# Layer 0 of a four-layer convolution kernel: planes without border rows, packed taps, results phase by phase, and sums in row halves

## The reference, cut to what matters

```python
base = conv1x1(x, w_qkv)                                  # 192 -> 576 channels
qkv = concatenate([dwconv(base, w_dw3, 1), dwconv(base, w_dw5, 2),
                   dwconv(base, w_dw7, 3)], axis=1)        # depthwise, 3 x 576 channels
qkv = conv1x1(qkv, w_pconv)                                # 1728 -> 576 channels
q, k, v = split(qkv, 3)                                    # 8 heads of 24 channels
q, k = l2norm(q), l2norm(k)                                # over the 4096 pixels
attn = einsum('bhcn,bhdn->bhcd', q, k) * temperature
# three softmaxes over the top 12, 16 and 18 of 24, mixed, times v, then w_proj
```

## Time and profile before

| | |
|---|---|
| median of 3 runs | 3204.47 us |
| profiled execution, its own time | 3192.12 us |
| its span (first to last instruction) | 3190.3 us |
| PE busy | 2387.6 us (75%) |
| DVE busy | 1220.4 us (38%) |
| ACT busy | 978.0 us (31%) |
| POOL busy | 812.5 us (25%) |
| transfers | 314.40 MB, mean 99 GB/s |
| mean granted clock of TensorE | 0.862 |

### The profile page before, as it was taken

The page is one execution under the profiler, slowest core; times in us unless marked ns, Lnnn a source line. Parts: engine busy times, 40 slices in busy tenths (PEclk is TensorE's granted clock), DMA queues, the critical chain, the costliest instruction groups (busy, mean ns, idle before and its releaser), DMA issues. The chain is left out here.

```text
span 3190.3 us, 37429 instructions
## 1 busy us (share of the span) xinstructions
PE 2387.6 (75%) x15968; PEld 1379.6 (43%) x15968; DVE 1220.4 (38%) x1081; ACT 978.0 (31%) x1264; POOL 812.5 (25%) x321
## 2 busy tenths in 40 slices
PE   3877878739999999995697938678677877877022
PEld 1566666627777777772352112223132212321022
DVE  4333434310000000004402160799499728974722
ACT  2344444410000000002210011666367526650400
POOL 1433334300000000000000000578188607870310
PEclk9989989869999999997795565799899989998556
DMA  5899999962122112102000110000000000002389
GB/s 180 273 296 310 292 302 283 267 225 86 49 90 90 65 70 90 45 1 84 9 1 29 46 48 20 0 0 0 0 1 0 0 0 1 0 16 66 107 226 272
DMA packets 175035, 314.40 MB, mean 99 GB/s; under 512 B 7049, under 2 KB 130185, under 8 KB 166217
## 3 DMA queue, kind: packets, MB, share of 16 engines
q1 hardware_dynamic: 162216, 305.94, 31.4%
q10 hardware_dynamic: 12672, 6.29, 0.7%
HBM read 185.59 MB, written 125.04 MB: 97 GB/s over the span
## 5 line engine op out<-in xcount | busy, mean ns | idle before, releaser
L589 PE MATMUL ps<-mem 128*128 128x288 f16 x5376 | 677.0, 286 | 50.9 <-DMA mem<-depthwise_out 50.9
L589 PEld LDWEIGHTS ps<-mem 128*128 128x128 f16 x5376 | 519.3, 98 | 194.5 <-issue 66.5
L1350 POOL TENSOR_TENSOR mem<-mem 128x1024 f32<-128x1024 f32 x48 | 113.1, 2356 | 1632.9 <-ACT mem L1340 1632.9
L1353 POOL TENSOR_TENSOR mem<-mem 128x1024 f32<-128x1024 f32 x192 | 448.3, 2353 | 40.8 <-ACT mem L1324 40.5
L434 PE MATMUL ps<-mem 56*96 56x256 f16 x5184 | 325.7, 288 | 105.8 <-DVE mem L527 96.4
L1298 PE MATMUL ps<-mem 128*128 128x512 f32 x768 | 379.3, 617 | 16.1 <-POOL mem L1353 13.2
L434 PEld LDWEIGHTS ps<-mem 56*96 56x96 f16 x5184 | 312.0, 130 | 127.4 <-DVE mem L527 102.8
L1381 DVE TENSOR_TENSOR_SCAN mem<-mem,ps 128x1024 f32<-128x1024 f32 x144 | 337.9, 2347 | 60.7 <-ACT mem L1331 37.2
L804 DVE MEMSET mem<- 96x96 f32 x2 | 0.3, 138 | 860.9 <-DMA mem<-in_tri 860.9
L527 DVE TENSOR_TENSOR mem<-ps,mem 96x1024 f16<-96x1024 f32 x144 | 171.3, 1217 | 274.6 <-ACT mem L472 274.6
L503 POOL TENSOR_TENSOR mem<-mem 120x2304 f16<-120x2304 f32 x36 | 163.7, 4548 | 342.0 <-ACT mem L465 342.0
(11 more groups left out here) (179 smaller groups left out, 2392.2 us busy)
## 6 DMA issues: line engine op xcount, KB each, us to landing
depthwise_out<-mem SPq DMA_DIRECT2D x36, 1536.0 KB, 15.6
mem<-depthwise_out SPq DMA_DIRECT2D x16, 3328.0 KB, 10.9
mem<-in_wd SPq DMA_DIRECT2D x40, 1080.0 KB, 17.4
mem<-base_phases SPq DMA_DIRECT2D x72, 504.0 KB
base_phases<-mem SPq DMA_DIRECT2D x56, 576.0 KB, 10.5
mem<-l_planes SPq DMA_DIRECT2D x48, 252.0 KB
mem<-in_x SPq DMA_DIRECT2D x4, 2048.0 KB, 10.9
l_planes<-mem SPq DMA_DIRECT2D x2, 4032.0 KB, 13.3
```

Source lines behind the costliest of these rows:

```text
L589: ins = nc.tensor.matmul(ps[:, 2 * (i % 2) + h, 0:HALF], d, pw[0:rows, wa, k, HALF * h:HALF * h + HALF], start=(k == 0 and n == 0), stop=( ...
L1353: nc.gpsimd.tensor_tensor(hh[:, n % 4, :], hh[:, n % 4, :], cs[:, n % 2, :], ALU.mult).then_inc(hc_pool, 1)
```

## The change

In layer 0's depthwise stage
- planes have 128 elements and no border rows (a row of 4 planes is 1024 instead of 1152 bytes). The matmuls for o = 0 and o = 2 leave out the block row that lies outside (240 instead of 256 columns) and come behind o = 1;
- taps are sent as 192 instead of 288 columns per channel pair: 96 for o = 1 and the 96 that are not zero in o = 0 and o = 2. Two transfers over 56 partitions each replace one over 120. ACT and POOL spread them with four instructions each where there was one. DVE clears the rest once;
- results are stored phase by phase, `[PHASES, 3 * QKV, 512]`, in three transfers over 32 partitions with runs of 16 KB;
- the second base matmul of each image uses only its 64 rows, and the two images' stand next to each other, on different rows of the array. The first 8 steps use three pairs of PSUM banks. In the loop the two steps of a batch stand ahead of units 0 and 2.

In the pointwise stage
- a piece comes in six transfers with runs of 1024 bytes; the last 64 rows are loaded twice, to both halves of the partitions, and the two output halves of the last row block use one half each;
- Gram sums are only q k'. DVE squares q and k of each block and adds the squares up; 8 matmuls with a column of ones behind the last block give the norms, and attention reads them.

Attention reads v in another order of phases. The diff, cut:

```diff
-        base_d = nc.dram_tensor("base_phases", [QKV, TAPROWS, PITCH], F16).ap()
-        d_dram = nc.dram_tensor("depthwise_out", [3 * QKV, PHASES, 4 * BLOCKS], F16).ap()
+        base_d = nc.dram_tensor("base_phases", [QKV, TAPROWS, PITCH0], F16).ap()
+        d_dram = nc.dram_tensor("depthwise_out", [PHASES, 3 * QKV, 4 * BLOCKS], F16).ap()
...
+    def base_before(n, k):
+        steps = base_steps(n)
+        return steps[k // 2:k // 2 + 1] if k % 2 == 0 else []
...
+    def base_psum(m, g, b):
+        return ps[0:width(m), (2 * (g % 3) if m == 0 else 0) + b, :]
...
             def load_taps(n):
-                sp.dma_start(w32[n % 2][0:64 + TAPROWS], inp["wd"][:, n * BP * YS * MD:(n + 1) * BP * YS * MD]).then_inc(w_loaded[n % 2], 16)
+                for t in range(2):
+                    sp.dma_start(w32[n % 2][64 * t:64 * t + TAPROWS], inp["wd"][TAPROWS * t:TAPROWS * (t + 1), n * BP * TAPS0:(n + 1) * BP * TAPS0]
+                                 ).then_inc(w_loaded[n % 2], 16)
...
             def store_out(n):
                 sp.wait_ge(dw_lo, UPB * (n + 1))
-                sp.dma_start(d_dram[6 * BP * n:6 * BP * (n + 1)].rearrange("(c k) f n -> (k f) c n", k=3), stg[n % 2][0:MD]
-                             ).then_inc(d_stored[n % 2], 16)
+                for k in range(3):
+                    sp.dma_start(d_dram[:, QKV * k + 2 * BP * n:QKV * k + 2 * BP * (n + 1)], stg[n % 2][PHASES * k:PHASES * (k + 1)]
+                                 ).then_inc(d_stored[n % 2], 16)
...
                 for b in range(B):
-                    nc.tensor.matmul(out, w[:, 0, c0:c0 + width(m)], xn[:, b, x], start=True, stop=False)
-                    nc.tensor.matmul(out, w[:, 1 + b, c0:c0 + width(m)], xn[:, 2, x], start=False, stop=True).then_inc(base_sum, 1)
+                    nc.tensor.matmul(base_psum(m, g, b), w[:, 0, c0:c0 + width(m)], xn[:, b, x], start=True, stop=False)
+                for b in range(B):
+                    p = slice(64 * b, 64 * b + 64)
+                    nc.tensor.matmul(base_psum(m, g, b), w[p, 1, c0:c0 + width(m)], xn[p, 2, x], start=False, stop=True).then_inc(base_sum, 1)
...
-                    for o in range(YS):
+                    for o in (1, 0, 2):
+                        lo, hi = 8 * (o == 0), BLOCKS - 8 * (o == 2)
...
             def taps(n):
+                src, dst = dense_taps(n)
+                nc.scalar.copy(dst[0], src).then_inc(w_hi, 1)
+                for q in range(3):
+                    src, dst = edge_taps(n, q)
+                    nc.scalar.copy(dst[0], src).then_inc(w_hi, 1)
...
-                src = d_dram[:, 2 * j:2 * j + 2, :].rearrange("c f n -> c (f n)")
-                sp.dma_start(dbuf[:, j % NSLOT, 0:NK - 1], src[0:128 * (NK - 1)].rearrange("(k p) n -> p k n", p=128)
-                             ).then_inc(d_loaded[j % NSLOT], 16)
-                sp.dma_start(dbuf[0:64, j % NSLOT, NK - 1], src[128 * (NK - 1):3 * QKV]).then_inc(d_loaded[j % NSLOT], 16)
+                for f in range(2):
+                    src, dst = d_dram[2 * j + f], dbuf[:, j % NSLOT, :, 512 * f:512 * f + 512]
+                    sp.dma_start(dst[:, 0:NK - 1], src[0:128 * (NK - 1)].rearrange("(k p) n -> p k n", p=128)).then_inc(d_loaded[j % NSLOT], 16)
+                    for h in range(2):
+                        sp.dma_start(dst[64 * h:64 * h + 64, NK - 1], src[128 * (NK - 1):3 * QKV]).then_inc(d_loaded[j % NSLOT], 16)
...
                         for h in range(2):
+                            rows = slice(64 * h, 64 * h + 64) if k == NK - 1 else slice(0, 128)
...
-                    pair = x[:, 0:2 * C].rearrange("p (a c) -> p a c", a=2)[:, :, h * HC:(h + 1) * HC]
-                    nc.tensor.matmul(ps[0:HC, 4 + 2 * b, 2 * HC * h:2 * HC * (h + 1)].rearrange("p (a c) -> p a c", a=2),
-                                     x[:, h * HC:(h + 1) * HC], pair, start=(f == 0 and h == 0), stop=(f == PHASES - 1), skip_group_check=True)
-                    ks = x[:, C + h * HC:C + (h + 1) * HC]
-                    ins = nc.tensor.matmul(ps[0:HC, 5 + 2 * b, HC * h:HC * (h + 1)], ks, ks,
+                    ins = nc.tensor.matmul(ps[0:HC, 4 + b, HC * h:HC * h + HC], x[:, h * HC:(h + 1) * HC], x[:, C + h * HC:C + (h + 1) * HC],
...
+                nc.vector.tensor_tensor(sq[:, i % 2], qkv[:, i % 2], qkv[:, i % 2], ALU.mult).then_inc(squared, 1)
+                dve.wait_ge(squared, i + 1)
+                nc.vector.tensor_tensor(sqsum[:, i % 2], sqsum[:, i % 2], sq[:, i % 2], ALU.add).then_inc(sq_added, 1)
```

More of the change, by code:

```diff
@@ L38 @@
 PITCH = 4 * PLANE
+PITCH0 = 4 * BLOCKS
+TAPS0 = 2 * MD
 SHIFTED = [0, 1, 2, 5, 6, 7]
@@ L278, in layer0_depthwise @@
     NM, NSTB, NWIN = 5, 4, 3
[L279 to L284, removed]
+    w = ar.take(2, QKV)
+    stb = ar.take16(NSTB, 4, PITCH0, dt=F16)
+    ext = ar.take16(len(SHIFTED), 4, PITCH0, dt=F16)
+    win = ar.take16(NWIN, BP, PITCH0, dt=F16)
+    WB = BP * YS * MD
+    w32 = [ar.take(BP * TAPS0) for _ in range(2)]
+    wh = [ar.take16(2 * WB + MD, dt=F16) for _ in range(2)]
     stg = [ar.take16(2 * BP, 4 * BLOCKS, dt=F16) for _ in range(2)]
     base_loaded = sem("l0_base_weights")
-    cleared = sem("l0_borders_cleared")
+    taps_cleared = sem("l0_taps_cleared")
     ext_cleared = sem("l0_shifted_cleared")
@@ L480, in _ @@
                     taps(n + 1)
-                for m, g in base_steps(n):
-                    base(m, g)
                 for k in range(UPB):
+                    for m, g in base_before(n, k):
+                        base(m, g)
                     unit(n, k)
@@ L551, in layer0_pointwise @@
     dbuf = dbuf.rearrange("p s (k n) -> p s k n", k=NK)
-    qkv = ar.take(2, QKV)
+    qkv = ar.take(2, 2 * C)
+    sq = ar.take(2, 2 * C)
+    sqsum = ar.take(B, 2 * C)
+    ones = ar.take(1)
     assert ar.at <= ar.size - NBLK * C
@@ L615, in _ @@
             gram(NBLK - 1)
+            pe.wait_ge(sq_added, NBLK)
+            for b in range(B):
+                for x in range(2):
+                    for h in range(2):
+                        c0 = C * x + HC * h
+                        ins = nc.tensor.matmul(ps[0:HC, 6, 4 * x + 2 * b + h:4 * x + 2 * b + h + 1], sqsum[:, b, c0:c0 + HC], ones,
+                                               start=(b == 0 and x == 0 and h == 0), stop=True, skip_group_check=True)
+            ins.then_inc(norm_sum, 1)
         @block.vector
@@ L805, in _ @@
             idb = bc(ident[P_, 0:HC].unsqueeze(1), [HC, BH, HC])
-            for x, lo in ((0, 0), (1, 2 * HC)):
+            if layer == 0:
+                step(V.tensor_copy(ssq[P_].rearrange("p x b -> p (x b)"), gacc[P_, 0, 0:2 * BH]))
+            for x, lo in ((0, 0), (1, 2 * HC)) if layer else ():
                 step(V.tensor_tensor(tmp[P_], gacc[P_, :, lo:lo + HC], idb, ALU.mult))
@@ L1644, in layouts @@
     wq = v["L0_conv_w_qkv"].T
-    wide = np.zeros((128, 3, QKV), f)
-    wide[:, 0] = wq[0:128]
-    wide[0:64, 1] = wq[128:192]
-    wide[64:128, 2] = wq[128:192]
-    o["wbase"] = wide
-    dws = [v["L0_conv_w_dw3"][:, 0], v["L0_conv_w_dw5"][:, 0], v["L0_conv_w_dw7"][:, 0]]
-    wd = np.zeros((64 + TAPROWS, QKV // 2, YS, MD), f)
+    o["wbase"] = np.stack(packed_rows(wq), 1)
+    dws = [v["L0_conv_w_dw3"][:, 0], v["L0_conv_w_dw5"][:, 0], v["L0_conv_w_dw7"][:, 0]]
+    wd = np.zeros((2, TAPROWS, QKV // 2, TAPS0), f)
+    place = {(1, q, ro): 32 * q + 8 * ro for q in range(3) for ro in range(4)}
+    for q in range(3):
+        for m in range(q + 1):
+            place[0, q, m] = MD + 16 * (0, 1, 3)[q] + 8 * m
+            place[2, q, 3 - q + m] = MD + 16 * (0, 1, 3)[q] + 8 * (q + 1) + 8 * m
     rows = [(0, p, r) for p in range(8) for r in range(4)]
```

119 lines of the change are left out of this document (74 added, 45 removed).

## The result

The changed kernel takes 3112.98 us, the median of 4 runs (3108.74 to 3119.63). The kernel before, run beside it, takes 3206.25 (4 runs, 3198.21 to 3219.32). The ratio is 0.9707, with a 95% interval of 0.9669 to 0.9745: faster by 93 us. The profiled execution took 3110.42 us, span 3107.6, against 3192.12 and 3190.3 before, 82.7 less in the span. The forecast of 3123 is 10 us off, and its sum of -81.5 stands against -82.7. (The medians differ by 93 and the traces by 83, because the profiled execution before is a quick one: it lies under all four runs.

The account below looks back on a forecast made before the run. Transfers were taken to bound layer 0's depthwise loop and PE its pointwise stage. Terms: -11 - 7 + 1.5 - 64 - 1 = -81.5 us; 3204 - 81 = 3123 us, range 3035 to 3190.

Parts of the forecast that it names:

- Pointwise blocks: Layer 0's pointwise stage: row halves save 0.36 us and Gram sums 0.64 per block, 64 us over 64 blocks.
- First base sums: Before the depthwise loop, 47 to 95 us: row halves, shorter waits and earlier weights save 11 us, bounds 3 and 13.
- Start of pointwise: First loads of the pointwise stage: shorter runs and more bytes lose 1.5 us, from 0.6 to 3.
- The rest, from the Gram copy on: End of pointwise and attention: added norm work against dropped copies and DVE operations, together -1 +/- 2 us.
- the loop: Layer 0's depthwise loop: fewer bytes at 242 GB/s, 13.1 us per batch, 552 to 545 us, gain 7.
- rival 2: Depthwise loop: bytes decide, rate stays 288 GB/s; loop -69 us, total -143, 3061; chance 0.18.
- Two base steps apart instead of together: Depthwise loop, PE: adds two tiling drains to a batch, 0.5 us, hidden behind the transfers.
- SP's three extra starts: Depthwise loop, SP's queue: 0.4 to 1 us each, covered; up to 3 us per batch if the cover went.
- 1 (217 GB/s, nothing overlaps): Depthwise loop: slow transfers run one behind the other at 217 GB/s; loop +48 us, total -26, 3178; chance 0.20.
- 4 (184 and 207): Depthwise loop: stores over 32 partitions at 184 GB/s, loads at 207; loop +108 us, total +34, 3238; chance 0.07.
- 3 (long runs lift the rate): Depthwise loop: taps and results at 391 GB/s, windows at 215; loop -115 us, total -190, 3015; chance 0.15.
- 5 (the row halves don't run together): Pointwise and first base sums: no overlap for 128 weight columns or f32; +23 and +7 us; no chance of its own.

Follow-up runs that it names:

- the added block: Changed kernel plus a block that only moves data between layer 0's depthwise and pointwise stages, run once; its total isn't a timing; whole batches ran at 306 and 293 GB/s.
- the three pairs of kernels that differ in it: Results in three stores over 32 partitions against one over 96: 3112.98 and 3100.82, 3034.78 and 3024.51, 3029.32 and 3011.63 us.

## Why the prediction was right, and where it was not

**Right, with the mechanism.**
- Pointwise blocks: -64 forecast. From the first matmul to the Gram copy it is 740.84 us before and 677.09 after, -63.8. Both halves of the term are shown by undoing them: row halves 22.5 (23 forecast), and the Gram sums 0.64 us per block in the trace (the forecast's 0.64; putting products back cost 0.68 per block).
- First base sums: -11 forecast, windows issued at 85.53 instead of 95.33, -9.8. The f32 row halves, which no row had shown, run together: 1.13 us for the two calls of L450, where two over all rows (L447) take 1.98. But a step went from 3.44 to 2.97 us, so the halves bring 0.47 and not 0.86 of it, 4 us in 8 steps where 6.9 were put down; the two calls over all rows stand 0.96 apart now and not 0.86, and why isn't shown. In return the first matmul starts 3.2 us sooner (50.57 for 53.73), where 2 were estimated.
- Start of pointwise: +1.5 forecast, +1.0 measured (from in_pw's issue to the first matmul 40.4 and 41.45). The rest, from the Gram copy on, is +2.3 (1753.3 and 1755.6), a little outside the -1 +/- 2 of the forecast; it holds layers 1 to 3 and comes to 1752 to 1762 us in most of the other traces, so this term can't be judged.

**Right as a number, wrong inside: the loop.** Forecast from 552 to 545, measured from 560.4 to 547.9 between the first windows and in_pw. (The trace of the kernel before with its store cut has 573.2, so the loop's gain is known only as 12 to 25 us.) The term failed in two places, and by less in a third.
- *The rate of a batch without base sums was mis-sized.* "I take 242: it is the nearest row" made it 13.1 us; it is 11.1, from 13.7 before, and 177.5 instead of 218.4 us for 16 such batches, with another 11 in the last stretch. As bytes over time that is 3.711 / 13.7 = 271 GB/s before and 3.179 / 11.1 = 286 after. So here rival 2 holds: bytes decide, and three stores over 32 partitions change little. The nearest row had been chosen by its partitions. Both have loads and stores at the same time, but layer 3's stretch has twice as many bytes loaded as stored (252 KB and 256 KB issues, 48 and 24 of them) and stores in packets of some 500 bytes, where this loop has as much in each direction and 16 KB runs. Which of these keeps it at 242 isn't shown. The slow slices that the forecast read as narrow transfers had mostly one direction: x was loads alone (208), the planes of the earlier trace rows were stores alone (217), and in the slow slices of the earlier trace rows at least three quarters of the bytes, by the sizes of the packets, were loads. The whole batch with loads and stores in equal parts ran at 293 to 306 GB/s in the added block, whatever the width.
- *A step was counted as hidden that wasn't.* "Two base steps apart instead of together add two such drains to a batch, 0.5 us by that row, hidden here" looked only at PE. SP's queue was not followed: the second base store stands in SP's queue ahead of windows, results and taps, and now waits for a step made half a batch later. The working had the next taps queued behind SP's starts, but put nothing on this wait. Batches with base sums became 19.4 us where 17.7 were implied (13.1 + 73 / 16) and 17.0 stood before: +39 us in the loop. Making the steps together again gives 40 us, moving the store 78. The other 38 us of those 78 are no part of what the change cost: the kernel before had such a wait too (76.0 us), but no run moved its store.
- *SP's three extra starts* were put at nothing with "up to 3 us per batch" if the cover went. The store's two are worth 10 to 18 us in all, or 0.3 to 0.5 per batch, in the three pairs of kernels that differ in it (12, 10 and 18), whatever the cause: not quite covered.

The errors cancel, and that is luck. The forecast's 545 us are 283 for the 16 batches with base sums and 262 for the other 20; measured are 310.7 and 237.3 (177.5 and the rest, 59.8), 28 more and 25 less. With the rate alone right (36 x 11.1 + 73 = 473 us) the forecast would have been 3051, near rival 2's 3061 and some 60 us too low. The share of the transfers was also forecast as still near 1; it is 0.86, and that was the sign to look at first. One sum in the prediction is off by 3: 486 is 66 below 552, not 69, so rival 2 would stand at 3064.

**The other rivals.** 1 (217 GB/s, nothing overlaps) and 4 (184 and 207) fall, as do their mechanisms: narrow stores next to narrow loads reach 301 to 306, and the kernel before with three stores is unchanged. 3 (long runs lift the rate) falls for the stores of this change: 263 GB/s with 16 KB runs, 266 with 1 KB. 5 (the row halves don't run together) falls for both kinds.

The Trainium skill (SBUF — State Buffer, "Can I just issue two DMAs to hit both halves?") says that two transfers, one on each half of the partitions, serialize. For loads this case agrees: 213 GB/s against 207 alone. For stores it does in part: layer 3's two stores on the halves ran at 217, and sixteen in turn began at 226 but reached 429. For a load on one half and a store on the other it doesn't: 301 GB/s. Here the measurement decides, and rival 1's 217 GB/s for a queue that mixes both directions makes its time 40% too long (306 measured).

## What to carry to other kernels

When an edit moves work later on one engine, find the instruction in an issuing queue that waits for that work, and count everything queued behind it; spreading the two steps cost 40 us here, and taking the store out of the way gave 78. Put stores whose data comes late behind the loads and stores that are ready. Take the rate for a mix of transfers from a stretch with the same mix (how much goes each way, and in what runs), not from one that shares only the partitions; if there is none, measure it alone first. And where the busy share of the transfers has fallen, look for a wait in the queue that issues them.

## What the hardware showed that was not expected

- A load and a store over 64 partitions overlap even on the same partitions: 305 GB/s against 207 and 206 alone. Over all 128 partitions both directions together give 424, no more than one alone (431 and 433).
- Stores on the two halves in turn speed up over their run, from 226 and 223 GB/s (725 to 735 us) to 426 and 429 (750 to 760 us), while loads on the two halves stay at 212 to 216 throughout. Why stores do and loads don't is open.
- The busy share of the DMA engines is 1.00 at 206 GB/s and at 424: it shows that transfers are under way, not how fast they run.
- Two matmuls with f32 operands on the two row halves run together, as those with f16 do: 1.13 us for the pair of 512 columns in the first base sums, against 1.98 for two over all rows.
